# Attention with 32-row fp32 score tiles instead of stacked bf16 parts, on one Trainium2 core

## The reference

```python
def _L0_cond_ref(x, mask, Wq, Wo):          # x (16, 256, 512), mask (16, 512), NH = 8, dk = 32
    q = jnp.transpose(x, (0, 2, 1)) @ Wq.T
    qh = q.reshape(B, T, NH, dk).transpose(0, 2, 1, 3)
    scores = scale * jnp.einsum('bhqd,bhkd->bhqk', qh, qh)
    logits = (scores * cmask + (1.0 - cmask) * NEG) * rmask     # mask over keys, then over rows
    attn = jax.nn.softmax(logits, axis=-1)
    ctx = jnp.einsum('bhqk,bhkd->bhqd', attn, qh)
    return jnp.transpose(ctx.transpose(0, 2, 1, 3).reshape(B, T, D) @ Wo.T, (0, 2, 1))
x = x + _L0_cond_ref(x, cond_2048, L0_cond_Wq, L0_cond_Wo)
x = x + conv(x); x = x + gru(cond_2048, x); x = x + _L3_cond_ref(x, ...)
```

## Time and profile before

| | us |
|---|---|
| median of 3 runs (lowest, highest) | 3395.29 (3395.16, 3397.47) |
| the profiled execution, whole | 3392.88 |
| its span, first to last instruction | 3390.9 |
| PE busy in the span | 2980.2 (88%) |
| DVE, ACT, POOL busy | 1965.2, 1313.4, 825.0 |

### The profile page before, as it was taken

How to read it: one execution, slowest core, us unless ns; L and a number is a source line. 1 busy time by engine, 2 the same in 40 slices (tenths; PEclk the granted TensorE clock), 3 DMA queues, 4 the chain that set the end, 5 groups by cost and what they waited for, 6 DMA issues and landing times. The chain is left out here.

```text
span 3390.9 us, 118705 instructions
## 1 busy us (share of the span) xinstructions
PE 2980.2 (88%) x48152; PEld 1741.9 (51%) x48152; DVE 1965.2 (58%) x4248; ACT 1313.4 (39%) x2323; POOL 825.0 (24%) x814
## 2 busy tenths in 40 slices
PE   3899999999469999999999999839989999998983
PEld 1344444444258888888888888713323333332320
DVE  3455545544277666676767673457666666666650
ACT  0455555555201111111111111115666666666663
POOL 2122222221001111121212121112334333333422
PEclk9899999999789999999999999968999999999997
DMA  3454455443400000000000000034455544555522
GB/s 113 129 161 137 128 160 144 143 138 88 111 2 0 0 0 0 1 0 0 0 1 0 0 0 0 4 109 130 136 158 158 147 142 145 154 140 156 153 67 61
DMA packets 185824, 281.66 MB, mean 83 GB/s; under 512 B 28646, under 2 KB 126726, under 8 KB 179458
## 3 DMA queue, kind: packets, MB, share of 16 engines
q1 hardware_dynamic: 185698, 280.26, 28.9%
HBM read 176.65 MB, written 103.53 MB: 83 GB/s over the span
## 5 line engine op out<-in xcount | busy, mean ns | idle before, releaser
L1285 DVE TENSOR_REDUCE x<-bank 128x1 f32<-128x512 f32 x1024 | 644.0, 683 | 348.3 <-PE bank L1354 347.3
L1209 ACT ACTIVATE x<-exp_ps 128x1024 f32<-128x1024 f32 x512 | 508.2, 1020 | 260.6 <-PE exp_ps L1328 258.6
L803 PE MATMUL exp_ps<-region,gru_hT 128*16 128x128 f32 x16384 | 495.6, 273 | 0.7 <-DVE gru_hT L893 0.7
L803 PEld LDWEIGHTS exp_ps<-region,gru_hT 128*16 128x16 f32 x16384 | 431.5, 103 | 20.3 <-DVE gru_hT L893 1.6
L1354 PE MATMUL bank<-region 100*128 100x512 bf16 x1024 | 407.2, 400 | 35.1 <-DMA region<-mask_rows 23.4
L470 ACT ACTIVATE l_probs<-exp_ps 128x512 f32<-128x512 f32 x512 | 297.5, 600 | 274.9 <-PE exp_ps L576 264.6
L1328 PE MATMUL exp_ps<-region 103*128 103x512 bf16 x1024 | 397.9, 395 | 1.5 <-DMA region<-max_scratch 1.0
L737 POOL TENSOR_TENSOR xT<-xT,gru_hT 128x64 f32 (+1 forms) x256 | 133.8, 523 | 998.8 <-DVE gru_hT L893 652.2
L838 ACT ACTIVATE gru_r<-exp_ps 128x128 f32<-128x128 f32 x256 | 71.0, 277 | 751.8 <-PE exp_ps L803 751.8
L865 DVE SCALAR_TENSOR_TENSOR xT<-x,condT,xT (+1 forms) x480 | 358.2, 795 | 1.1 <-issue 1.1
L527 DVE TENSOR_REDUCE l_maxes<-bank 128x1 f32<-128x512 f32 x352 | 237.0, 690 | 198.4 <-PE bank L604 198.2
(11 more groups left out here) (127 smaller groups left out, 3837.3 us busy)
## 6 DMA issues: line engine op xcount, KB each, us to landing
region<-parts_scratch SPq DMA_DIRECT2D x128, 384.0 KB
key_query_scratch<-x SPq DMA_DIRECT2D x192, 256.0 KB, 3.4
region<-key_query_scratch SPq DMA_DIRECT2D x64, 768.0 KB
parts_scratch<-l_parts SPq DMA_DIRECT2D x128, 256.0 KB, 3.2
l_rden<-rden_scratch SPq DMA_DIRECT2D x64, 256.0 KB
l_out<-x_scratch SPq DMA_DIRECT2D x64, 192.0 KB
l_xin<-in_x SPq DMA_DIRECT2D x16, 512.0 KB, 5.4
l_rden<-rden_scratch SPq DMA_DIRECT2D x128, 64.0 KB, 2.0
```

What stands on the lines that cost most here:

```text
L803: last = pe.matmul(out[QW * j:QW * j + rows, cols], hT[:, p, k, 0:rows], wh[:, k, j, gate, :], start=False, stop=True, skip_group_check=True)
L1209: act.activation(probs[:, 2 * (seg % 2) + hp, :, :], exp_ps[slot % 2][:, :, :], ACT.Exp)\
L1285: dve.tensor_reduce(maxes[:, half, qt, head % HH:head % HH + 1], tasks.bank(n)[:, :], AX_X, ALU.max)\
```

## The change

The stack, its bf16 parts, the stores and loads through DRAM of parts and maxima, and the splitting of `kq` on ScalarE and GpSimd are gone. Projection results are evacuated by ScalarE into `qu`, from which VectorE makes the masked `kq`, in one half of four heads at a time ("q0", "q1"); `kq` is kept twice and is used by TensorE directly as both operands. One head is 32 partitions of it. `products` writes, in each slot: the fp32 scores of two heads (32 rows, 128 columns, 512 queries), the fp32 maxima products of two other heads on the other 64 partitions, and then for each of the two score tiles a bf16 product of four rows that adds the key mask and minus the row maximum. All are written to PSUM pairs of two banks, and scores, maxima and the other tasks now share one ring of three pairs (39 tasks a step). The exponential and the maximum's reduction take a pair (1024 values) in one instruction. Maxima are split into three bf16 parts by VectorE in a layout of 32 columns per head (`spread`), GpSimd copies the row mask into the fourth column, TensorE turns them, and ScalarE copies the turned rows to `max_rows`. The values are the transposes of `qu` ("v0", "v1"). The output is one task of a pair. The GRU's weights are loaded by ScalarE's DMA queue at the start of the block.

Cut to its core:

```diff
+    AT = {"mtb": 1, "q1": 3, "v1": 5, "mta": 10, "q0": 11, "v0": 13, "out": 15, "reciprocal": 5, "sums": 10}
     SCALE = (9, 12)
     SEGS = 8
-    LOADS = 6
-    PLACES = ((0, 4, 5, 7), (1, 3, 6), (2,))
-    WINDOW = (4, 5, 0, 2)
-    STORES = 8
+    NPART = 4
...
+        qu = sb("l0_qu", [P, T], F32)
+        kq = sb("l0_kq", [P, 2, CC, T], F32)
...
+        pairs, o_ps, d_ps = g.exp_ps + [g.bank45], g.bank[6], g.bank[7]
...
+            order += [(slot, "st", slot, 0, 16), (slot, "max", slot, 1, 16)]
+            for kind, off in (("mtb", 0), ("q1", 1), ("v1", 1), ("mta", 1), ("q0", 2), ("v0", 2), ("out", -1)):
+                if AT[kind] == slot:
+                    order.append((slot, kind, 0, off, 1))
...
+            return slot // 8, slot % 8 // 2, 1 - slot % 2
...
-            def load_stack(s, par, half, before):
-                hs = slice(GH * half, GH * half + GH)
-                wait(sp, stack_loaded[half], before)
-                for w, at in enumerate(WINDOW):
-                    sp.dma_start(stack[0:AUG, par, w, hs, :],
-                                 g.parts_dram[at:at + 3].rearrange("t (r h) n -> (t r) h n", h=H0)[:, hs, :]).then_inc(stack_loaded[half], 16)
-                for w, row in ((0, 0), (1, 1)):
-                    sp.dma_start(stack[AUG:AUG + 1, par, w, hs, :],
-                                 g.rows[row, bass.ds(s, 1), :].rearrange("a (o n) -> a o n", o=1)
-                                 .broadcast_to([1, GH, T])).then_inc(stack_loaded[half], 16)
-            def store_max_rows(par, half, made, read, stored):
-                wait(sp, mp_done, made)
-                wait(sp, mrow_loaded[half], read)
-                sp.dma_start(g.mrow_dram[half, :, 0:GH, :].rearrange("p h n -> h p n"), max_parts[:, :, :])\
-                  .then_inc(mrow_stored, 16)
-                wait(sp, mrow_stored, stored)
-                sp.dma_start(stack[KMAX:KALL, par, 1, GH * half:GH * half + GH, :], g.mrow_dram[half, :, 0:GH, :])\
-                  .then_inc(mrow_loaded[half], 16)
...
+            load_x(0)
+            for n, w in enumerate((g.l0_wq, g.l0_wo)):
+                sp.dma_start(w_raw[:, n, :].rearrange("p (m c) -> p m c", m=CC),
+                             w.rearrange("(m p) c -> p m c", m=CC)).then_inc(w_loaded, 16)
+            load_mask(0)
+            sp.wait_ge(rows_set, 1)
+            load_keys(0, 0)
...
+                if active(s, 1):
+                    wait(sp, ready["st"], n(16, 0))
+                if active(s, 2) and not (isinstance(s, int) and s == -2):
+                    wait(sp, ready["q1"], n(1, 2))
+                    load_x(s + 2)
+                    wait(sp, kq_done[1], n(1, 2))
+                    load_mask(s + 2)
+                if active(s, 1) and not (isinstance(s, int) and s == -1):
+                    load_keys(s + 1, 1 - par)
...
-            sp.wait_ge(st_ready, TILES * (LAST + 1))
-            for w, dram, gates in zip(gru_weights(g), (g.l2_wi, g.l2_wh), ((0, 2, 1), (0, 2, 1))):
-                for k in range(TC):
-                    for slot, gate in enumerate(gates):
-                        sp.dma_start(w[:, k, :, slot, :],
-                                     dram[k * P:k * P + P, gate * T:gate * T + T].rearrange("p (j f) -> p j f", f=P))\
-                          .then_inc(g.gru_w_loaded, 16)
...
-            def split_max(n, kind, need):
-                wait(pool, mp1_done, n + 1)
-                wait(pool, taken[kind], need)
-                pool.tensor_tensor(max_parts[:, 1, :], neg_max[:, :], max_parts[:, 0, :], ALU.subtract).then_inc(mp_chain, 1)
-                wait(pool, mp_chain, 2 * n + 1)
-                pool.tensor_tensor(neg_max[:, :], neg_max[:, :], max_parts[:, 0, :], ALU.subtract).then_inc(mp_chain, 1)
-                wait(pool, mp_chain, 2 * n + 2)
-                pool.tensor_tensor(max_parts[:, 2, :], neg_max[:, :], max_parts[:, 1, :], ALU.subtract).then_inc(mp_done, 1)
+            pool.memset(g.x1[:, :, :, 0:PAD], 0.0).then_inc(pad_set, 1)
+            def set_masks(half, kind, b):
+                count = b
+                if not isinstance(b, int):
+                    count = pool.snap(pool.to_reg(b))
+                wait(pool, ready[kind], count)
+                if not isinstance(b, int):
+                    b = pool.snap(pool.to_reg(count + 0))
+                pool.tensor_copy(spread[:, half, :, :, 3:4],
+                                 g.condT[:, :, bass.ds(b, 1)].rearrange("p k (o u) -> p k o u", u=1).broadcast_to([P, TC, GH, 1]))\
+                    .then_inc(masks_set[half], 1)
             def step(s, par):
-                if active(s, 0):
-                    split_max(2 * s + 1, "mtb", s + 1)
-                if active(s, 2):
-                    wait(pool, part1_done, s + 3)
-                    pool.tensor_tensor(kq[:, :, :], kq[:, :, :], parts[:, 0, :, :], ALU.subtract).then_inc(res1_done, 1)
-                    wait(pool, res1_done, s + 3)
-                    wait(pool, part2_done, s + 3)
-                    pool.tensor_tensor(parts[:, 2, :, :], kq[:, :, :], parts[:, 1, :, :], ALU.subtract).then_inc(part3_done, 1)
...
+            def evac_max(half, kind, b):
+                wait(act, ready[kind], b + 1)
+                wait(act, ready["st"], 16 * b - 8 * (1 - half))
+                act.activation(max_rows[:, half, :], tasks.bank_of(kind)[:, 0, :].bitcast(BF16)[:, 0:T], ACT.Copy)\
+                   .then_inc(taken[kind], 1)
...
+            def evac_q(idx, kind, b):
+                wait(act, ready[kind], b + 1)
+                wait(act, kq_done[1 - idx], b + idx)
+                wait(act, ready["v1" if idx == 0 else "v0"], b + idx)
+                act.activation(qu[:, :], tasks.bank_of(kind)[:, 0, :], ACT.Copy).then_inc(taken[kind], 1)
...
-                        for hh in range(2):
-                            tile = 2 * slot + hh
-                            wait(act, st_ready, TILES * s + tile + 1)
-                            act.activation(probs[:, 2 * (seg % 2) + hp, hh, :], exp_ps[tile % 3], ACT.Exp, scale=scale)\
-                               .then_inc(exp_done, 1)
+                        wait(act, ready["st"], 16 * s + slot + 1)
+                        act.activation(probs[:, 2 * (seg % 2) + hp, :, :], tasks.bank_of("st", slot)[:, :, :], ACT.Exp, scale=scale)\
+                           .then_inc(taken["st"], 1)
...
+            act.wait_ge(x_loaded, 16)
+            for w, dram, gates in zip(gru_weights(g), (g.l2_wi, g.l2_wh), ((0, 2, 1), (0, 2, 1))):
+                for k in range(TC):
+                    for slot, gate in enumerate(gates):
+                        act.dma_start(w[:, k, :, slot, :],
+                                      dram[k * P:k * P + P, gate * T:gate * T + T].rearrange("p (j f) -> p j f", f=P))\
+                           .then_inc(g.gru_w_loaded, 16)
...
+                n = 2 * b + half
+                m = maxes[:, half, :, :]
+                part = lambda i: spread[:, half, :, :, i]
+                wait(dve, taken["max"], 16 * b + 8 * (half + 1))
+                wait(dve, ready[kind], b)
+                dve.tensor_copy(part(0), m).then_inc(split_chain, 1)
+                wait(dve, split_chain, 4 * n + 1)
+                dve.tensor_tensor(rest[:, :, :], m, part(0), ALU.subtract).then_inc(split_chain, 1)
+                wait(dve, split_chain, 4 * n + 2)
+                dve.tensor_copy(part(1), rest[:, :, :]).then_inc(split_chain, 1)
+                wait(dve, split_chain, 4 * n + 3)
+                dve.tensor_tensor(rest[:, :, :], rest[:, :, :], part(1), ALU.subtract).then_inc(split_chain, 1)
+                wait(dve, split_chain, 4 * n + 4)
+                dve.tensor_copy(part(2), rest[:, :, :]).then_inc(split_done, 1)
...
+                        dve.tensor_reduce(maxes[:, half, qt, 2 * hp:2 * hp + 2], tasks.bank_of("max", slot)[:, :, :], AX_X, ALU.max)\
+                           .then_inc(taken["max"], 1)
+                        if slot % 8 == 7:
+                            split(half, "mtb" if half else "mta", s + 1)
...
+                at = {kind: next(n for n, t in enumerate(tasks.tasks) if t[1] == kind and t[2] == slot) for kind in ("st", "max")}
+                if active(s, 0):
+                    if slot % 8 == 0:
+                        wait(pe, taken["mtb" if grp else "mta"], s + 1)
+                        wait(pe, keys_loaded, 16 * (s + 1))
+                    tasks.free(pe, s, at["st"])
+                    for i in range(2):
+                        rows = slice(QW * (2 * hp + i), QW * (2 * hp + i) + QW)
+                        pe.matmul(tasks.bank(at["st"])[:, i, :], kq[rows, par, grp, kt * P:kt * P + P], kq[rows, par, grp, :],
+                                  start=True, stop=False)
+                if active(s, 1):
+                    half, qt, mp = max_tile(slot)
+                    if slot % 8 == 0:
+                        wait(pe, kq_done[half], s + 2)
```

(32 more changed lines are left out.)

242 lines of the change are left out of this document (80 added, 162 removed).

## The result

The changed kernel takes 3452.14 us (median of 4 runs, 3448.28 to 3454.51). The kernel before, timed beside it, takes 3396.38 us (4 runs, 3395.16 to 3401.22). The ratio is 1.016, with a 95% interval of 1.0143 to 1.0178: slower by 56 us, where +11 was forecast.

A forecast was written before the change was run, and what follows sets the result against it. TensorE was taken as full before, with a new wait for the exponential after: +41 us in the steps, -22 at the start and -8.5 at the end gave +11, 3406 us; summed bounds 3380 to 3439, stated range 3360 to 3465.

The forecast's parts named there:

- the chain: First attention: even slot's scores, exponential, odd slot's maxima in the same pair, weighted sums; 5.20 us per two slots against 4.58.
- the range: Whole kernel: 3360 to 3465 us, leaving out the rival without parallel row tiles and part of the fast one.
- the staggered rival: Row tiles' weight loads go one after another, second tile 0.22 us late; +3.5 us a step, 3460 us; chance 0.18.
- The clock: TensorE might drop to half clock because it pauses every second slot, doubling the 4.5 us of products in two slots.
- The set of four row tiles, 0.88: First attention's steady step: four fp32 tiles, two scores and two maxima, run side by side by rows in 0.88 us.
- The small tasks: Each step: projection halves 3.44 us, values 0.88, free turning +0.22, other 0.3, output 5.24, five shape changes 0.45.
- What hid: Work removed from ScalarE, GpSimd and SP hid under a full TensorE, gives nothing in the steady part; added work costs nothing.
- Start and end: First scores at about 73 us against 95.3, -22 us; block's end without SP issuing the weights, -8.5 us.
- The GRU and the second attention do not change.: Stages after the first attention: no change in time, 0 us in the sum.
- The argument put against it: Against staggering by weight loads: eight loads of 32 columns are out within the time of one.
- Row tiles not running at once: Rival: scores and maxima 1.76 us each, at least +43 us a step, about 4070 us; chance 0.05.
- The covered wait: Rival: the ring's wait does not bite, two slots 4.7 us, a step 48.1, kernel 3343 us; chance 0.14.

The follow-up runs named there:

- Half an exponential: Changed kernel with the exponential of only one of the two heads of each pair, 512 of 1024 values; 3398.91 us, ratio 1.0009 to the kernel before.
- the second run: Changed kernel with the GRU's 24 weight loads issued by SP behind its first loads, not by ScalarE; 3414.74 us, ratio 1.0048 to the kernel before.
- the last run: Changed kernel with weighted sums cut in two, sums evacuated ahead of the exponentials in slots 2 and 10, GRU weights issued by SP; 3325.78 us, ratio 0.9788 to before.
- the run with split sums: Changed kernel with weighted sums cut in two, values products after even slots, ones products after odd slots; 3453.6 us, ratio 1.0161 to the kernel before.

## Why the prediction came out as it did

The direction, the chain and the range held; 45 us of the loss were not in the sum. That the range held was luck: by its own bounds the sum reached up to 3439 us, and 3452 lies above. The range went on to 3465 only to take in the staggered rival, whose mechanism did not occur. The direction is no luck: without the second attention's 25.5 us the kernel would still be slower by some 30.

**What bounds the kernel, and the chain.** Right. A step is the sum of TensorE's distances plus one wait per two slots (0.46 us; about 0.6 was forecast). Half an exponential gave 0.43 us of 0.42, and with the wait filled the step is below that of before. The clock, named as a way to be wrong, stayed at 1.00 from 120 to 800 us in spite of these pauses.

**The set of four row tiles, 0.88.** Mis-sized. It measured 0.97 (525.71 to 526.68, with 0.53 between its passes instead of 0.44), and it stands in the chain twice: 528.17 to 529.23 is 1.06, 0.97 and the change of shape of 0.09. Eight times 5.37 instead of 5.20 is +1.4 us a step. I took the figure of the column tiles in the stream for tiles that start fresh after another shape or a wait. The Trainium skill ("TensorE: Matmul & The Clock Gate", "Measured speedup vs the span model") gives 3.07 times for four row tiles. By that figure the set would be 1.15, an estimate; here four products of 0.88 in 0.97 are 3.6 times, and the measurement decides.

**The small tasks.** Mis-sized by 0.5 in sum. Projection halves 1.92 each with the change of shape (515.98 to 517.90; I had 1.72 and 0.09), values 0.59 (I had 0.44 and 0.09), turning 0.33 (0.30), output 5.44 (499.47 to 504.91; I had 5.24 and 0.09); slots 10 and 11 take 0.22 more than the others, as forecast. Together 8 x 5.37 + 3.84 + 1.18 + 0.33 + 5.44 + 0.22 = 54.0, which is what the trace has, where I had 52.1: +4.4 us a step against 49.6, above the forecast's own upper bound of 4. From the second turned maxima of the first step to those of the last, fifteen steps, after takes 805.2 us (80.8 to 886.0) and before 740.7 (101.5 to 842.2). That is +64.5 where 38 + 1.3 was forecast, and these 25 us are nearly all of the 27 by which this stretch missed.

**What hid.** Right. VectorE's reduction of 1024 takes 1.23 us (I took 1.3) and delays nothing; ScalarE is busy 284 of 680 us. That GpSimd's and SP's removed work gave nothing in the steady part was not tried by itself; it follows from TensorE's terms, which account for the whole step.

**Start and end.** Right: 72.74 against 73, and the 8.5 us came. The weights on ScalarE's queue cost 10 us of the start, as the second run shows.

**"The GRU and the second attention do not change."** This step failed, by 25.5 us and the largest single amount. I argued from the instructions alone, which are the same; the runs show that it hangs on the length of SP's program ahead of the loop, which the change had shortened, and that each turn of the loop (two steps) cost SP 8 us more, in front of the denominators. That is 20 to 21 of the 25.5; the rest is untraced, as are the 4.6 us by which the GRU's stretch became shorter.

**The rivals.** The staggered rival's number (3460) is the nearest to the result, but its mechanism didn't occur: all four tiles start within 20 ns (525.71 to 525.73), not 220 apart. A small part of its kind did, the 0.09 per fresh set. The argument put against it was too strong by its own row: 1024 loads in 33.4 us are 0.26 us for eight, not the 0.11 of one. Row tiles not running at once is excluded by the run that puts scores and maxima on the same rows, 1.82 us instead of 0.96. The covered wait, with 48.1 us a step, is what the last run made (47.55).

## What to carry to other kernels

Products that become shorter move the bound from TensorE's sum to the buffer that comes free last: write down, per slot, which bank a product needs and who frees it, and put independent products in that gap before judging the change. When one wait is filled, look for the evacuation that was early enough only because of it, and at the stages that lack the filling work. When a stage that nobody touched gets slower, compare the queues' holes at the loop's turn, and the instruction packets in the stretch of the loop (the page's total misleads: before has 82, none of them there), before thinking about its data.

## What the hardware showed that I had not expected

**A loop's turn can cost 8 us more, by the length of the program ahead of it.** SP's pause at the turn of the second attention's loop is 1.95 to 2.3 us in before and in the kernels with a longer SP program, and 10.2 to 10.5 us in after, five times, once in a turn of two steps. With that pause packets move on the queue of instructions, four of them from 2730 to 2760 us in after; before has none there. They come from 2748 us on. Until then, from the start of the pause at 2743.8, data fill 90% and more of the DMA engines' time, and half of it from 2748 to 2750; whether the instruction packets wait for these data was not tried. This looks like the loop's code being loaded again at each turn, when it lies unluckily. Shown is that the length of SP's program decides it and that instruction packets go with it; which property of the place matters was not tried.

**Row tiles.** Four fp32 tiles of 32 rows and 128 columns on different rows start within 20 ns. The second weight load of the same rows starts 0.11 us after the first (525.82 against 525.71), and a fresh set's second pass is 0.09 late. That the one makes the other was only argued. The Trainium skill ("TensorEngine Tiling (Array Packing)", "Key Properties") says that different tiles can load weights and multiply in parallel; the starts of this trace agree.

**The clock.** In the run with split sums the granted clock fell from 1.00 to 0.50 in the step without maxima and stayed there from 855 to 915 us, although TensorE was busy 58.2 of these 60 us. A pause of 1.75 us stands in front of the fall, but 25 pauses of up to 1.9 us left the clock at 1.00 from 180 to 820 us of the same kernel. So the length of a pause did not tell here when the clock falls. From the last turned maxima to the last exponential this kernel takes 30 us more than after, whose clock in that stretch is 0.89 on the mean.
